# A four-layer transformer tower: stages of the layers put in another order, the FFN input cut in two

## The reference

```python
for i in range(L):                                    # L = 4
    nx = t5_layer_norm(h, ln1[i])                     # w * x * rsqrt(mean(x*x) + 1e-6)
    q, k, v = nx @ attn_q[i], nx @ attn_k[i], nx @ attn_v[i]        # 12 heads of 64
    scores = jnp.einsum('bqhd,bkhd->bhqk', q, k) + bias
    attn = jax.nn.softmax(scores, axis=-1)
    ctx = jnp.einsum('bhqk,bkhd->bqhd', attn, v).reshape(b, s, H * DK)
    h = h + ctx @ attn_o[i]
    nx = t5_layer_norm(h, ln2[i])
    y = jax.nn.relu(nx @ ffn_wi[i]) @ ffn_wo[i]       # F = 768
    if i in (1, 3):                                   # 8 experts, the top 2 weighted by softmax
        y = y + moe_ffn(nx.reshape(-1, d), gate_w[mi], moe_w1[mi], moe_w2[mi]).reshape(b, s, d)
    h = h + y
return t5_layer_norm(h, ln_f)
```

## Time and profile before

| | |
|---|---|
| Median of three runs | 789.63 us |
| Profiled execution, its span | 791.12 us, 789.3 us |
| Busy: PE, DVE, ACT, POOL | 92%, 56%, 52%, 45% |
| Mean granted TensorE clock | 0.948 |
| Weights read from HBM and all else | 47.70 MB |

### The profile page before, as it was taken

One profiled execution on the slowest core, in us unless ns is written; L12 is line 12 of the kernel. 1 busy time (PEld: TensorE's weight loads), 2 busy tenths in 40 slices (PEclk: granted clock), 3 DMA queues, 4 the chain that ended last, 5 costly groups with the idle time before them and its releaser, 6 DMA issues.

```text
span 789.3 us, 16416 instructions
## 1 busy us (share of the span) xinstructions
PE 727.2 (92%) x6751; PEld 647.2 (82%) x6751; DVE 438.7 (56%) x917; ACT 407.3 (52%) x913; POOL 351.6 (45%) x327
## 2 busy tenths in 40 slices
PE   6887899889899989899999999998999998999995
PEld 4763478778778979899999878787789888999995
DVE  0337535376265475466656645652664854666664
ACT  1467335536255344377767355352554445766642
POOL 3346525474565340255765334435662503355420
PEclk9977899999998999899999999979989998999998
DMA  7221001021221201053444020012212002423300
GB/s 206 81 71 41 2 2 32 1 81 42 73 68 32 71 2 56 13 154 112 141 140 141 11 72 2 1 42 74 68 32 71 24 35 70 127 76 107 101 1 22
DMA packets 36610, 49.21 MB, mean 62 GB/s; under 512 B 6155, under 2 KB 27575, under 8 KB 36023
## 3 DMA queue, kind: packets, MB, share of 16 engines
q1 hardware_dynamic: 33259, 43.49, 19.2%
q10 hardware_dynamic: 3276, 4.67, 1.9%
HBM read 47.70 MB, written 0.45 MB: 61 GB/s over the span
## 4 chain that ended last, share of the span: by engine, by line
PE 66%; DVE 10%; ACT 9%; POOL 8%; issue 3%; DMA 2%; SPq 0%; POOLq 0%; ACTq 0%; DVEq 0%
PE pd L682 34%; PE pa L682 20%; PE ps L682 9%; PE pa L713 4%; POOL w L611 3%; POOL wqkv L611 2%; ACT wide L1020 2%; POOL prob L620 2%; DVE mx L1060 1%; DVE prob L1213 1%; ACT wqkv L932 1%; ACT pa L1021 1%; DVE rc L1065 1%; DVE xn L1100 1%; ACT w L932 1%
## 5 line engine op out<-in xcount | busy, mean ns | idle before, releaser
L611 POOL TENSOR_TENSOR w<-raw,w 128x384 fp32r<-128x384 f32 x140 | 142.4, 1019 | 122.9 <-ACT w L932 115.1
L682 PE MATMUL pd<-wide,w 128*128 128x264 f32 x1200 | 156.0, 286 | 0.0
L682 PEld LDWEIGHTS pd<-wide,w 128*128 128x128 f32 x1200 | 149.3, 188 | 0.8 <-DVE wide L1236 0.5
L682 PE MATMUL pa<-xs,w 128*128 128x264 f32 x810 | 127.8, 301 | 8.7 <-DVE wide L1236 4.2
L682 PEld LDWEIGHTS pa<-xs,w 128*128 128x128 f32 x810 | 114.0, 202 | 13.1 <-DVE wide L1236 5.8
L1236 DVE TENSOR_TENSOR wide<-pa,wide 128x264 fp32r<-128x264 f32 x144 | 61.9, 431 | 40.3 <-ACT pa L1021 38.4
L620 POOL TENSOR_TENSOR prob<-prob,mx 66x792 f32<-66x792 f32 x36 | 54.8, 1527 | 63.2 <-DVE mx L1060 63.0
L682 PE MATMUL ps<-xs,w 128*128 128x264 f32 x480 | 77.6, 293 | 3.1 <-DVE prob L1213 3.1
L682 PEld LDWEIGHTS ps<-xs,w 128*128 128x128 f32 x480 | 67.9, 197 | 4.4 <-DVE prob L1213 2.9
L1020 ACT ACTIVATE wide<-pa 128x264 fp32r<-128x264 f32 x144 | 56.9, 395 | 27.5 <-PE pa L682 27.4
L632 POOL TENSOR_TENSOR rs<-var,exponent 88x3 f32<-88x3 f32 x22 | 18.6, 848 | 114.0 <-DVE var L1082 114.0
(11 more groups left out here) (125 smaller groups left out, 1204.1 us busy)
## 6 DMA issues: line engine op xcount, KB each, us to landing
raw<-in_moe_w_dram SPq DMA_DIRECT2D x16, 576.0 KB, 4.1
raw<-in_moe_w_dram SPq DMA_DIRECT2D x16, 384.0 KB, 3.5
raw<-in_moe_w_dram SPq DMA_DIRECT2D x32, 192.0 KB, 4.0
vtok<-cw_rows ACTq DMA_DIRECT2D x4, 1056.0 KB, 5.9
raw<-in_attn_o_dram SPq DMA_DIRECT2D x4, 576.0 KB, 4.0
raw<-in_ffn_wo_dram SPq DMA_DIRECT2D x4, 576.0 KB, 4.0
vtok<-in_patches_dram SPq DMA_DIRECT2D x2, 768.0 KB, 8.0
raw<-in_attn_q_dram SPq DMA_DIRECT2D x4, 384.0 KB, 3.7
```

The costliest lines, as they stand in the source:

```text
L611: ins = nc.gpsimd.tensor_tensor(low, whole, high.bitcast(F32), ALU.subtract)
L682: return nc.tensor.matmul(out_ap, lhsT, rhs, start=first, stop=last)
```

## The change

Only the list and what counts its entries is changed; all matmuls, activations and splits stay, except for warm matmuls (dense layer: one, three and six instead of three times two; expert layer: two and two added, four taken away).

- `hid` becomes two stages of three groups each. They stand one behind the other but in one place: for expert 1 of half 0 the output projection of half 1 and its squares are between.
- In a dense layer the transposes and `pv` of half 1 move up around `o_tail`, `o_main` and the norm, the last `pv` ahead of `hid`; of the four splits that ended the layer, q's stands behind `hid`, k's behind the next norm, v's and o's in the next layer.
- In an expert layer v's split stands behind the norm of half 1 between the two `qk`, o's in the place of w1's; w1 and w2 of block 0 and of block 1 come later, one at a time.
- `logits` of half 0 goes from the scores' loop to behind `hid`; of half 1 it comes behind `y_main` of expert 1, without warm matmuls ahead.

```diff
+    def hid(hf, layer, blk):
+        yield ("hid", hf, layer, blk, 0)
+        yield ("hid", hf, layer, blk, 1)
...
+            yield ("tp", 1, layer, 0)
             yield ("o_tail", 0, layer)
-            yield ("tp", 1, layer, 0)
+            yield ("pv", 1, layer, 0)
+            yield ("tp", 1, layer, 1)
             yield ("scores_end", 1, layer)
             yield ("o_main", 0, layer)
             yield ("fold", 0, layer, "o")
             yield ("squares", 0, "ln2")
-            yield ("pv", 1, layer, 0)
-            yield ("tp", 1, layer, 1)
+            yield from warm(1)
+            yield ("pv", 1, layer, 1)
+            yield ("tp", 1, layer, 2)
             yield ("norm", 0, "ln2", layer)
-            yield ("pv", 1, layer, 1)
-            yield from warm(2)
-            yield ("scale", 0, "ln2", layer)
-            yield ("split", None, "qkv", layer + 1, 0)
-            yield ("tp", 1, layer, 2)
-            yield from warm(2)
             yield ("pv", 1, layer, 2)
             yield ("tp", 1, layer, 3)
-            yield from warm(2)
-            yield ("hid", 0, layer, 0)
-            yield ("split", None, "qkv", layer + 1, 1)
+            yield from warm(3)
+            yield ("scale", 0, "ln2", layer)
             yield ("pv", 1, layer, 3)
+            yield from warm(6)
+            yield from hid(0, layer, 0)
+            yield ("split", None, "qkv", layer + 1, 0)
             yield from y(0, layer, 0)
-            yield ("split", None, "qkv", layer + 1, 2)
             yield ("fold", 0, layer, "ffn")
             yield ("squares", 0, "ln1")
             yield ("o_tail", 1, layer)
             yield ("norm", 0, "ln1", layer + 1)
+            yield ("split", None, "qkv", layer + 1, 1)
             yield from warm(4)
...
-            yield ("split", None, "o", layer + 1, 0)
             continue
 
         yield ("qk", 0, layer, 0)
         yield ("norm", 1, "ln2", layer - 1)
+        yield ("split", None, "qkv", layer, 2)
         yield ("qk", 0, layer, 1)
...
-            if b in (0, 2):
-                yield ("split", None, "w1" if b == 0 else "w2", layer, 0)
-        yield ("hid", 1, layer - 1, 0)
+            if b == 0:
+                yield ("split", None, "o", layer, 0)
+        yield from hid(1, layer - 1, 0)
...
         yield ("tp", 0, layer, 1)
+        yield ("split", None, "w1", layer, 0)
         yield ("y_main", 1, layer - 1, 0)
         yield ("fold", 1, layer - 1, "ffn")
         yield ("squares", 1, "ln1")
+        yield from warm(2)
         yield ("pv", 0, layer, 1)
         yield ("tp", 0, layer, 2)
         yield ("norm", 1, "ln1", layer)
+        yield from warm(2)
...
         yield ("pv", 0, layer, 3)
-        yield from split_block(layer, 1)
         yield from warm(6)
         yield ("qk", 1, layer, 0)
+        yield ("split", None, "w2", layer, 0)
...
             yield ("v", 1, layer, b)
-            if b == 2:
-                yield ("logits", 0, layer)
-        yield ("hid", 0, layer, 0)
+        yield from hid(0, layer, 0)
+        yield ("logits", 0, layer)
         yield ("tp", 1, layer, 0)
         yield ("scores_end", 1, layer)
+        yield ("split", None, "w1", layer, 1)
...
         yield ("tp", 1, layer, 2)
+        yield ("split", None, "w2", layer, 1)
...
         yield ("pv", 1, layer, 3)
-        yield ("hid", 0, layer, 1)
+        yield ("hid", 0, layer, 1, 0)
         yield from o(1, layer)
         yield ("squares", 1, "ln2")
+        yield ("hid", 0, layer, 1, 1)
+        yield ("norm", 1, "ln2", layer)
         yield ("y_tail", 0, layer, 1)
-        yield ("norm", 1, "ln2", layer)
+        yield ("scale", 1, "ln2", layer)
         yield ("y_main", 0, layer, 1)
-        yield ("scale", 1, "ln2", layer)
-        yield from warm(4)
         yield ("logits", 1, layer)
...
-        H_GROUPS = {"hid": KT}
+        H_GROUPS = {"hid": KT // 2}
```

More of the change, by code:

```diff
@@ L282, in stages @@
         yield ("pv", 1, layer, 3)
-        yield ("hid", 0, layer, 1)
+        yield ("hid", 0, layer, 1, 0)
         yield from o(1, layer)
         yield ("squares", 1, "ln2")
+        yield ("hid", 0, layer, 1, 1)
+        yield ("norm", 1, "ln2", layer)
         yield ("y_tail", 0, layer, 1)
-        yield ("norm", 1, "ln2", layer)
+        yield ("scale", 1, "ln2", layer)
         yield ("y_main", 0, layer, 1)
-        yield ("scale", 1, "ln2", layer)
-        yield from warm(4)
         yield ("logits", 1, layer)
-        yield ("hid", 1, layer, 0)
+        yield from hid(1, layer, 0)
         yield ("split", None, "w1", layer, 2)
@@ L297, in stages @@
         yield ("cw_in", 1, layer)
-        yield ("hid", 1, layer, 1)
+        yield from hid(1, layer, 1)
         for blk in range(2, last + 1):
-            yield ("hid", 0, layer, blk)
+            yield from hid(0, layer, blk)
             if blk < last:
@@ L304, in stages @@
             if blk < last:
-                yield ("hid", 1, layer, blk)
+                yield from hid(1, layer, blk)
                 yield ("split", None, "w2", layer, blk + 1)
@@ L312, in stages @@
         yield ("squares", 0, "ln1" if layer + 1 < LAYERS else "final")
-        yield ("hid", 1, layer, last)
+        yield from hid(1, layer, last)
         ending = ("ln1", layer + 1) if layer + 1 < LAYERS else ("final", 0)
@@ L509, in hidden_after @@
         def hidden_after(y_stage, k):
-            return groups_after(H_GROUPS, ("hid",) + y_stage[1:]) - KT + k + 1
+            return groups_after(H_GROUPS, ("hid",) + y_stage[1:] + (1,)) - KT + k + 1
         def probs(u):
@@ L866, in _ @@
                 elif name == "hid":
-                    layer, blk = stage[2:4]
-                    if blk == 0:
+                    layer, blk, part = stage[2:5]
+                    if blk == part == 0:
                         pe.wait_ge(x_ready, x_ready_after(("scale", hf, "ln2", layer)))
-                    pe.wait_ge(chunk_split, chunks_until("w1", layer, blk))
+                    if part == 0:
+                        pe.wait_ge(chunk_split, chunks_until("w1", layer, blk))
                     w = w1[ffn_no(layer, blk) % 2]
-                    for m in range(KT):
+                    for m in range(part * KT // 2, (part + 1) * KT // 2):
                         product(bank_h()[:, 0:NT], split_pairs(w[:, 0], w[:, 1], xs[hf], slice(m * 128, (m + 1) * 128)), h_full)
@@ L927, in high_part @@
                 elif kind == "w1" and ffn_no(layer, i) >= 2:
-                    act.wait_ge(h_full, groups_after(H_GROUPS, ("hid", 1) + FFN[ffn_no(layer, i) - 2]))
+                    act.wait_ge(h_full, groups_after(H_GROUPS, ("hid", 1) + FFN[ffn_no(layer, i) - 2] + (1,)))
                 elif kind == "w2" and ffn_no(layer, i) >= 2:
@@ L1015, in _ @@
                     gate_fn = ACT.Gelu if stage[3] else ACT.Relu
-                    for m in range(KT):
+                    for m in range(stage[4] * KT // 2, (stage[4] + 1) * KT // 2):
                         n = hid_no.next() - 1
```

## The result

The changed kernel takes 764.72 us in the median of 4 runs (760.59 to 767.22), the kernel before 788.69 (787.08 to 790.37, 4 runs): ratio 0.968 [0.964, 0.971], faster by 24.0 us. The forecast was 763, range 754 to 776. Medians and ranges are over all executions of a kernel, while the ratios leave out slow ones, which lie over 1.5% above that kernel's fastest. The profiled execution is the fastest of the four, 760.59 us for a span of 758.8, so its stages add up to more gain (30.5 us of span) than the medians show.

A forecast was written before the change was run, and what follows sets the result against it. TensorE, busy 92% of 789.3 us, bounds the kernel, so only its idle and half-speed time can be won. Stretches sum to -30.1, less 3.4 for two clock falls: -26.7, 764.4 or 763 from the median, range 754 to 776.

The forecast's parts named there:

- A: End of a dense layer up to the FFN input: 15.1 us, +0.45 in layer 0, -1.75 in layer 2.
- the rival of moving half-speed time: Half-speed time moves to other places instead of going: sum -12, 778 us; chance 0.13.
- B: From a dense layer's FFN input to the next layer's first projection: 16.65 us, -3.5 in layer 0, -5.3 in layer 2.
- E: Expert layer, stretch up to half 1's projection: 19.0 us in layer 1, -2.1 there and in layer 3.
- C: Projections up to the first `v`: the 0.77 us wait goes, 10.9 us, -0.75 in each layer.
- the slower rival: V's split comes late and holds up every `v`, needing 13.3 us of lateness per layer: 792 or so; chance 0.04.
- D: Expert layer's score loop, shorter split between the first two subtractions of maxima: -1.1 us in layer 1, -0.3 in layer 3.
- G: The router's stretch in an expert layer: 20.5 us, -4.4 in layer 1, -1.5 in layer 3.
- H: H1 and H2 together, around expert 1's hidden tiles and half 1's FFN input: -3.5 us in each pair.
- H1: Expert 1's hidden tiles and half 1's o: 14.5 us, -1.7, with the scale about 1.15 us late.
- H2: Stretch with half 1's FFN input, behind H1: 6.4 us, -1.8, with 1.5 us of new PSUM bank waits.
- only idle time moves: Rival: the change moves only idle time, stretches being set by an overlooked ScalarE-VectorE chain: 788 to 790 us; chance 0.02.

The follow-up runs named there:

- its repeat: The changed kernel once more, with only a comment added at its end: 765.42 us, ratio 0.972 to the kernel before.
- the two late ones: Edits of the changed kernel: half 1's logits behind that half's FFN input (767.9 us), and the same with the routing weights' transfers later too (771.28 us).

## Why the prediction was right, step by step

Of the 24 us, the splits are the largest part: 11.7 us alone, and 19 when taken out of the whole (784.1 against 764.7 and 765.4). Undoing the logits' move costs 4.4 us by its own stages, undoing the new order around expert 1's FFN input 6.4 by its stages and 6.5 by the median (against 765.1). The added warm matmuls and the dense attention's order give nothing that the medians can tell. The parts don't add up, for two reasons that the windows show: the clock falls in other stages each time, and a split beside x costs more in the new order. In A q's split cost 0.54 us of wait in the kernel before and 2.12 in the new order, both at clock 1.00.

*A* (15.1 forecast): 15.46 in layer 2; 18.10 in layer 0, the one stage that became slower. The work was sized to 0.4 us, with some luck: the forecast left out the wait of 0.54 us for x that rows 3 holds and gave no reason. It went because q's split no longer runs beside x, which the forecast nowhere counts. The clock was not sized: this is the rival of moving half-speed time, in one place, and close to the 3.4 us set aside. With ten warm matmuls in the changed kernel's places A took 17.7 us or more in 10 of 12 stretches (this profile, its repeat, the edits of logits, of FFN input, and the two late ones); with q's split back beside them the clock fell in 1 of 2 (0.82 and 1.00); with six in the new order A fell in 1 of 4; with pairs around the norm in none of 4. That the number or place decides is argued from counts, not shown, and no median separates them.

*B* (16.65): 16.79 and 16.61. The wait for the power was put at 0.55 and is 0.39, that for x at 1.4 and is 1.09, with two subtractions of 1.13 beside GpSimd. Busy time was put at 14.7 and is 15.24 and 15.03, so that the total is closer than its terms. The Trainium skill's rule (GPSIMD Engine Reference, Specifications) on contention with two SBUF inputs held in the place where the prediction applied it, and twice more where it did not: the 1.49 us in E and the 2.12 in A with the splits back.

*C* (10.9): 10.58. V's split ends 0.3 us ahead of the first `v`; the slower rival needed 13.3 us of lateness and got none. The margin was thinner than the forecast's 0.5.

*D and E* (32.5 and 32.0): 32.80 and 31.62. The size was right and E's reason half right. I charged E's gain to half-speed time and that to the splits. With the splits back and the warm matmuls kept the clock stays at 1.00 in both layers, and the stretch is still 2.5 us longer, by the wait for x and D's longer split. In the kernel before, x's chain in E ran beside GpSimd's pieces just as slowly and ended when the projection began, at 257.05, but TensorE, at half speed, had work until then:

```profile
255.87 1.13 DVE L1072 TENSOR_TENSOR xs<-xn,xs 64x264 fp32r<-64x264 f32 x1
```

So the half-speed time had covered the wait. Full speed alone took E of layer 1 only from 21.14 to 20.67 us (with four warm matmuls more), and moving the splits took it from there to 19.27. The four warm matmuls (0.82 us) go with the clock: with them E kept it in every profile, 22 stretches, and without them it fell in both layers before and in one of two layers, twice, with the splits moved. D in layer 3 was put at -0.3 and is -1.1 (13.76 to 12.67), as in layer 1.

*G* (20.5): 20.04 and 20.89. TensorE has no wait at all in layer 1's stretch, and one of 0.67 us in layer 3's, for a copy of `v` by ScalarE ahead of the router. The 0.4 us left for ScalarE behind the router did not come: it was idle 1.95 us ahead of the exponential, as forecast, the copies of `tp` queued behind it, and `y_tail` covered them.

*H* (20.9): 20.47 in both. H1 is 14.02 where 14.5 was forecast: the late scale was put at 1.15 us, and its waits are 0.23 and 0.21. H2 is 6.45 where 6.4 was forecast, and that is luck: its half-speed time was put at 3.4 us and was 2.7 (8.21 to 5.52 busy), the bank wait at 1.5 and is 0.93, and the forecast's 4.8 + 1.5 makes 6.3.

*The sum*: the two pairs gave 12.9 and 15.9 us where 14.9 and 15.2 were forecast, 28.8 of 30.1. The allowance for returning half-speed time (3.4) was only partly needed here, for A's fall of layer 0 (2.6 against layer 2). The profile of the repeat, 764.66 us and so nearer the median, had A fall in both layers, 5.6 us over 15.46 together, and its two pairs gave 24.4 us where the forecast with its allowance had 26.7. So the allowance was of the right kind and somewhat small, and which stage would need it was not foreseen.

*TensorE's busy time* was forecast at 714 and is 706.8, 716.6 in the profile of the repeat; the first is the fastest of four executions, and its front part, with unchanged code, is 2.4 us shorter.

The rival "only idle time moves" fell with the first profile. No version tried is measurably faster than the changed kernel: 763.06, 762.97 and 763.78 against 764.7 and 765.4, with intervals that overlap.

Open: what decides a fall in A or F, and whether the logits' edit loses anything outside its own stages.

## What to carry to other kernels

Where a small instruction of a slow engine stands on the path of the busiest one, place the long work behind it, not ahead of it: here eight pieces ahead of a power cost 3.1 us of wait, and four ahead and four behind it 0.4 and 1.1. Look also at what that long work runs beside: GpSimd's pieces beside x's last subtractions cost TensorE 1.1 to 2.1 us wherever they met at full clock in the new order. Read the granted clock per stage before charging a stage's gain to it, since half-speed time can hide a wait that appears once it goes. And compare stage windows rather than medians when the edits are worth less than the 9 us and more by which executions of one kernel differ.

## What the hardware showed unexpectedly

The front part, the same code in all kernels run, took 170.0 to 185.1 us. In three profiles of fourteen it was above 180: two of those with six warm matmuls, and the late logits with late transfers. In these three the granted clock from 78 to 109 us was 0.50 to 0.53; in the other eleven it was 0.85 to 0.95. The window of the same 31 us in the changed kernel and in that with six warm matmuls in the dense layers alone (columns as in rows 3):

```profile
78.00:109.00 31.00, 29.25 (x416) 19.40 (x422) 13.35 (x32) 12.64 (x24) 11.97 (x9) 0.95 0.01 2
```

```profile
78.00:109.00 31.00, 30.58 (x238) 17.17 (x236) 10.54 (x23) 10.02 (x17) 10.49 (x8) 0.50 0.01 1
```

At clock 0.50 TensorE did 238 matmuls where it did 416 otherwise, with busy time near the whole stretch in both. The stages up to there are written alike in all of these kernels, and I can't tell what decides it.
